# Another order of the turn in a fused linear-attention and gated-FFN layer

## The reference, cut to what matters

```
x: 16 x 512 tokens x 256 channels, float32                      (16 blocks)
qkv = relu(x @ Wqkv.T)          q, k, v: 32 heads of 8 channels
vk  = per head: [v, 1].T @ k over the tokens of a block
num, den = vk applied to q ;    att = num / (den + 1e-15)
x1  = layernorm(x + att @ Wproj.T + bias)
h   = silu(x1 @ (Wg/127).T) * (x1 @ (Wu/127).T)       hidden 768
out = layernorm(x1 + h @ (Wd/127).T)
```

## Time and profile before

| | |
|---|---|
| median of the runs | 548.8 us |
| the profiled execution | 549.34 us |
| its span, first to last instruction | 547.5 us |
| mean granted TensorE clock | 0.998 |
| busy PE / DVE / ACT / POOL | 533.1 / 392.7 / 221.4 / 80.4 us |
| chain that ended last | PE 93%, DVE 4%, ACT 1% |
| DMA | 29.04 MB, mean 53 GB/s |

### The profile page before, as it was taken

How to read it: one execution, slowest core, us unless ns; L and a number is a source line. 1 busy time by engine, 2 the same in 40 slices (tenths; PEclk the granted TensorE clock), 3 DMA queues, 4 the chain that set the end, 5 groups by cost and what they waited for, 6 DMA issues and landing times.

```text
span 547.5 us, 9297 instructions
## 1 busy us (share of the span) xinstructions
PE 533.1 (97%) x3531; PEld 465.8 (85%) x3531; DVE 392.7 (72%) x885; ACT 221.4 (40%) x376; POOL 80.4 (15%) x94
## 2 busy tenths in 40 slices
PE   8889999999999999999999999999999999999995
PEld 4777989898898988989898898988989898898975
DVE  5777858587684957858587684957858587684976
ACT  3365243442525435243542524435243542524431
POOL 2001110011100111110011100111110011100212
PEclk9999999999999999999999999999999999999999
DMA  8400120202112030121202112030121202102011
GB/s 296 166 0 3 40 78 29 87 0 77 38 38 77 0 112 3 38 77 31 84 0 77 38 38 77 0 110 5 38 77 37 78 0 77 38 0 79 1 40 40
DMA packets 8653, 29.04 MB, mean 53 GB/s; under 512 B 960, under 2 KB 1728, under 8 KB 8640
## 3 DMA queue, kind: packets, MB, share of 16 engines
q1 hardware_dynamic: 8640, 28.85, 14.8%
HBM read 20.46 MB, written 8.39 MB: 53 GB/s over the span
## 4 chain that ended last, share of the span: by engine, by line
PE 93%; DVE 4%; ACT 1%; issue 1%; DMA 1%; POOL 0%; POOLq 0%; SPq 0%
PE abcd_ps L585 45%; PE gate_ps L585 17%; PE up_ps L585 16%; PE abcd_ps L625 6%; PE abcd_ps L633 5%; PE abcd_ps L614 3%; DMA wq_raw<-w_q 1%; DVE x1T_lo L337 0%; PE abcd_ps L732 0%; DVE h L344 0%; ACT silu L241 0%; DVE st L567 0%; DVE st L400 0%; DVE r L563 0%; DVE att L377 0%
## 5 line engine op out<-in xcount | busy, mean ns | idle before, releaser
L344 DVE SCALAR_TENSOR_TENSOR h<-up_ps,silu 128x512 f32<-128x512 f32 x96 | 66.1, 688 | 79.1 <-ACT silu L241 79.1
L241 ACT ACTIVATE silu<-gate_ps 128x512 f32<-128x512 f32 x96 | 57.4, 597 | 98.3 <-PE gate_ps L585 98.3
L585 PE MATMUL abcd_ps<-wd_hi,h_hi 128*128 128x256 f32 x384 | 93.1, 283 | 0.8 <-DVE h_lo L337 0.8
L585 PE MATMUL abcd_ps<-wd_hi,h_lo 128*128 128x256 f32 x384 | 92.9, 283 | 0.0
L585 PE MATMUL gate_ps<-x1T_hi,wg_hi 128*128 128x512 f32 x192 | 79.4, 414 | 2.0 <-DVE x1T_lo L337 1.9
L337 DVE TENSOR_TENSOR h_lo<-h,h_hi 128x512 fp32r<-128x512 f32 x96 | 66.1, 689 | 14.4 <-ACT h_hi L236 11.2
L585 PE MATMUL up_ps<-x1T_hi,wu_hi 128*128 128x512 f32 x192 | 75.1, 391 | 0.0
L585 PE MATMUL up_ps<-x1T_lo,wu_hi 128*128 128x512 f32 x192 | 75.0, 391 | 0.0
L585 PE MATMUL gate_ps<-x1T_lo,wg_hi 128*128 128x512 f32 x192 | 74.9, 390 | 0.0
L585 PEld LDWEIGHTS abcd_ps<-wd_hi,h_hi 128*128 128x128 f32 x384 | 73.7, 192 | 1.1 <-DVE h_lo L337 1.0
L585 PEld LDWEIGHTS abcd_ps<-wd_hi,h_lo 128*128 128x128 f32 x384 | 73.7, 192 | 0.0
(11 more groups left out here) (119 smaller groups left out, 945.2 us busy)
## 6 DMA issues: line engine op xcount, KB each, us to landing
x_raw<-x_tok SPq DMA_DIRECT2D x16, 512.0 KB, 3.2
xT_raw<-x_chan SPq DMA_DIRECT2D x15, 512.0 KB, 3.3
out<-out_sb SPq DMA_DIRECT2D x15, 512.0 KB, 2.6
wg_raw<-w_gate SPq DMA_DIRECT2D x1, 768.0 KB, 6.3
wu_raw<-w_up SPq DMA_DIRECT2D x1, 768.0 KB, 7.8
wd_raw<-w_down SPq DMA_DIRECT2D x1, 768.0 KB, 9.1
xT_raw<-x_chan SPq DMA_DIRECT2D x2, 256.0 KB, 3.6
wkv_raw<-w_kv SPq DMA_DIRECT2D x1, 512.0 KB, 5.5
```

Source lines behind the costliest of these rows:

```text
L241: nc.scalar.activation(silu[:, j % 2, :], gate_ps[j % 2][:], ACT.Silu, scale=WSCALE).then_inc(silu_ok[j], 1)
L344: nc.vector.scalar_tensor_tensor(out=h[:, j, :], in0=up_ps[j % 2][:], scalar=WSCALE, in1=silu[:, j % 2, :], op0=ALU.mult, op1=ALU.mult).th ...
L585: last = mm(dst, lhsT, rhs, start=start and n == 0, stop=stop and n == len(pairs) - 1)
```

## The change

PE does in turn i: pieces 0 to 3, the transposes of att, pieces 4 and 5, proj, q and all four kv tiles of block i+1, the first half of down, vk of block i+1, the second half of down, the transposes of x1, num of block i+1. So vk and num of a block are now made at the end of the turn before. Down sums into `gate_ps[1]` and `up_ps[1]`, q into A and B, kv into CC, D, A, B, x1T into `gate_ps[0]` and `up_ps[0]`. A piece j from 2 on waits for `silu_ok[j-2]` ahead of its gate products and for `h_ok[j-2]` only ahead of its up products. x1 is normalised in place in r1, transposed from there, and SP copies r1 to x1 with a transfer, for which the next `r1_of` waits. DVE's order follows: the output of block i-2 is written inside the FFN half, the low part of x transposed between h of tiles 2 and 3, the low parts of h of tiles 2 and 3 after those of att, those of 4 and 5 after r1. The four signals per kind for the last block's token tiles become one counter each.

```diff
@@ sync
+            def turn(i):
+                any_i = not isinstance(i, int)
+                if any_i or i >= 2:
+                    sp.wait_ge(out_ok, i - 1)
+                    sp.dma_start(out[i - 2], out_sb[:].rearrange("p t c -> p (t c)")).then_inc(stored, 16)
+                if any_i or i + 1 < NB:
+                    sp.wait_ge(xb_ok, i + 1)
+                    sp.dma_start(x_raw[:], x[i + 1]).then_inc(x_in, 16)
+                if any_i or i + 2 < NB:
+                    load_xT(i + 2)
+                if any_i or 0 < i < NB - 1:
+                    sp.wait_ge(r2_ok[1], i)
+                    sp.dma_start(x1[:], r1[:]).then_inc(x1_copied, 16)
@@ vector
             def r1_of(b, pairs=False):
+                if not isinstance(b, int) or b > 1:
+                    dve.wait_ge(x1_copied, 16 * (b - 1))
...
+            def ffn_half(i):
+                att_of(i)
+                h_of(i - 1, 0)
+                if not isinstance(i, int) or i > 1:
+                    out_of(i - 2)
+                h_of(i - 1, 1)
+                h_lo_of(i - 1, 0, 1)
+                h_of(i - 1, 2)
+                if not isinstance(i, int) or i < NB - 1:
+                    xT_lo_of(i + 1)
+                h_of(i - 1, 3)
+                attT_lo_of(i)
                 h_lo_of(i - 1, 2, 3)
                 h_of(i - 1, 4, 5)
+            def attention_half(i):
                 r1_of(i)
                 dve.wait_ge(st1_ok, i + 1)
+                h_lo_of(i - 1, 4)
+                aggregated(st1, mv1, mv1_ok)
+                h_lo_of(i - 1, 5)
+                x1_of(i, r1)
                 r2_add(i - 1, 0, x1)
                 dve.wait_ge(r2_ok[0], i)
                 stats(st2, r2, 0)
+                vk_of(i + 1)
                 r2_add(i - 1, 1, x1)
                 dve.wait_ge(r2_ok[1], i)
                 stats(st2, r2, 1, st2_ok)
                 dve.wait_ge(st2_ok, i)
+                x1T_lo_of(i)
                 aggregated(st2, mv2, mv2_ok)
@@ tensor, gate_up
                     if j >= 2:
-                        pe.wait_ge(h_ok[j - 2], b + 1)
+                        pe.wait_ge(silu_ok[j - 2], b + 1)
+                    if j == 1 and (not isinstance(b, int) or b > 0):
+                        pe.wait_ge(r2_ok[0], b)
+                        pe.wait_ge(r2_ok[1], b)
...
                     add_up(gate, gate_hi[:-1], stop=False)
+                    if j >= 2:
+                        pe.wait_ge(h_ok[j - 2], b + 1)
                     add_up(up, up_hi[:-1], stop=False)
@@ tensor
+            def ffn_half(i):
+                gate_up(i - 1, 0, 1, 2, 3)
                 attT_of(i)
                 gate_up(i - 1, 4, 5)
                 proj_of(i)
+            def attention_half(i):
+                pe.wait_ge(xT_lo_ok, i + 2)
+                q_of(i + 1)
+                for t, bank in enumerate((CC, D, A, B)):
+                    if t < 2:
+                        pe.wait_ge(r1_ok[t], i + 1)
+                    else:
+                        pe.wait_ge(q_ok[t - 2], i + 2)
+                    kv_of(t, i + 1, bank)
+                down_of(i - 1, (0, 1))
+                vk_of(i + 1)
+                down_of(i - 1, (2, 3))
+                x1T_of(i, r1)
+                num_of(i + 1)
```

More of the change, by code:

```diff
@@ L101, in build @@
         A, B, CC, D = (abcd[:, n, :] for n in range(4))
+        down_ps = (gate_ps[1][:], up_ps[1][:])
         num_ps = abcd[:, :, 0:KC * NW].rearrange("p t (k n) -> p t k n", k=KC)
@@ L130, in build @@
         rstd1_pair, x1_pair = signals("rstd1_pair", 2), signals("x1_pair", 2)
-        down_tile, r2_tile, st2_tile = signals("down_tile", NT), signals("r2_tile", NT), signals("st2_tile", NT)
-        mv2_tile, ve2_tile = signals("mv2_tile", NT), signals("ve2_tile", NT)
-        rstd2_tile, out_tile = signals("rstd2_tile", NT), signals("out_tile", NT)
+        down_tile, r2_tile, st2_tile, mv2_tile, ve2_tile, rstd2_tile, out_tile = (
+            signal(f"{n}_tile") for n in ("down", "r2", "st2", "mv2", "ve2", "rstd2", "out"))
         last_down = [bank[:, :C] for bank in (A, B, CC, D)]
@@ L173, in _ @@
             sp.dma_start(wd_raw[:], down_w).then_inc(wd_in, 16)
[L174 to L178, removed]
+            turn(0)
+            turn(1)
+            with sp.Fori(2, NB - 2) as i:
+                turn(i)
+            turn(NB - 2)
+            turn(NB - 1)
+            turn(NB)
             for t in range(NT):
-                sp.wait_ge(out_tile[t], 1)
+                sp.wait_ge(out_tile, t + 1)
                 sp.dma_start(out[NB - 1][:, t * C:(t + 1) * C], out_last[:, t, :]).then_inc(stored, 16)
@@ L268, in attT_hi_of, with x1T_hi_of @@
                 T_hi_of(b, attT_mm, attT_hi, attT_hi_ok, (A, B))
-            def x1T_hi_of(b, banks=(CC, D)):
+            def x1T_hi_of(b, banks=(gate_ps[0][:], up_ps[0][:])):
                 T_hi_of(b, x1T_mm, x1T_hi, x1T_hi_ok, banks)
@@ L390, in attT_lo_of, with x1T_lo_of @@
                 T_lo_of(b, attT_hi_ok, attT_lo_ok, attT_hi, attT_lo, (A, B))
-            def x1T_lo_of(b, banks=(CC, D)):
+            def x1T_lo_of(b, banks=(gate_ps[0][:], up_ps[0][:])):
                 T_lo_of(b, x1T_hi_ok, x1T_lo_ok, x1T_hi, x1T_lo, banks)
@@ L427, in r2_add @@
                 nc.vector.scalar_tensor_tensor(
-                    out=pair(r2, n), in0=(A, B)[n], scalar=WSCALE, in1=pair(x1_of_b, n), op0=ALU.mult, op1=ALU.add).then_inc(r2_ok[n], 1)
+                    out=pair(r2, n), in0=down_ps[n], scalar=WSCALE, in1=pair(x1_of_b, n), op0=ALU.mult, op1=ALU.add).then_inc(r2_ok[n], 1)
             def normed(dst, r, mv, rs, ok, tiles=range(NT)):
@@ L440, in out_of @@
             def out_of(b):
+                if not isinstance(b, int) or b > 0:
+                    dve.wait_ge(stored, 16 * b)
                 dve.wait_ge(rstd2_ok, b + 1)
@@ L504, in second_part @@
                 dve.wait_ge(st2_ok, i)
-                x1_of(i, x1)
+                x1T_lo_of(i)
                 aggregated(st2, mv2, mv2_ok)
[L507 to L524, removed]
-            i = NB - 1
[L528 to L537, removed]
+            for i in (1, 2):
+                ffn_half(i)
+                attention_half(i)
+            with dve.Fori(3, NB - 1) as i:
+                ffn_half(i)
+                attention_half(i)
+            i = NB - 1
+            ffn_half(i)
             h_lo_of(i - 1, 4, 5)
@@ L638, in attT_of, with x1T_of @@
                 transposed(att, (A, B), attT_mm)
-            def x1T_of(b, src, banks=(CC, D)):
+            def x1T_of(b, src, banks=(gate_ps[0][:], up_ps[0][:])):
                 pe.wait_ge(x1_ok, b + 1)
@@ L689, in down_of @@
             def down_of(b, tiles=range(NT)):
+                pe.wait_ge(h_ok[NH - 1], b + 1)
                 for t in tiles:
[L691 removed]
+                    last = down_part(b, t, range(NH), down_ps[t // 2][:, (t % 2) * C:(t % 2 + 1) * C])
                     if t % 2:
                         last.then_inc(down_mm[t // 2], 1)
[L695 to L718 removed]
+            def ffn_half(i):
+                gate_up(i - 1, 0, 1, 2, 3)
                 attT_of(i)
@@ L793, in _ @@
                     for t in (2 * n, 2 * n + 1):
-                        last = nc.tensor.transpose((CC, D)[k][:, t * P:(t + 1) * P],
+                        last = nc.tensor.transpose((A, B)[k][:, t * P:(t + 1) * P],
                                                    x1_last[:, t, k * P:(k + 1) * P], ident)
```

100 lines of the change are left out of this document (28 added, 72 removed).

## The result

The changed kernel is slower, by less than a per cent: a median of 554.2 us in nine runs (552.24 to 557.0) against 549.2 for the kernel before (547.83 to 551.16 in nine), a ratio of 1.0086 with a 95% interval of 1.0066 to 1.0106, so 3.6 to 5.8 us. The forecast was 552.2, +3.4; the range held it, and the sign was right. One execution of experiment 1, 664.14 us at a mean granted clock of 0.755, is left out of that run's ratio.

A forecast was written before the change was run, and what follows sets the result against it. PE, busy in all of a 32.83 us turn, was taken as the bound. Seams -2.5, wait of piece 0 +5.7 and ends +0.2 gave +3.4 on the median 548.8: 552.2 us, range 546.3 to 556.6.

The forecast's parts named there:

- The wait of piece 0: PE waits for x1T_lo behind num until 3.07 after the x1 transposes start (T): 0.41 us per turn, +5.7 us.
- The seams: PE's losses at products behind plain float32 groups: x1T and num share one, vk's gets narrower; -2.5 us in all.
- one seam for two: x1T and num stand together on PE, saving one loss of 0.13 in each of 14 turns, -1.8 us.
- The sign that was named: On PE, three first products of 0.5 us per turn and not four would show the saved seams.
- Rival 3: Seams don't merge, since the stop at piece 0 replaces them: 554.7 us, 1.1% slower, chance 0.10.
- The upper one of the wait: Upper bound at piece 0: 0.6 per turn (+8.4), if num ran at 0.117 per product with no hand-over.
- Slack 0.25. No cost: At proj: attT_lo lets it start at 14.73, PE arrives at 14.98; slack was 0.65 before; no cost, but tightest.
- Rival 1: Proj waits as well, the DVE and ACT chain from den to attT_lo being late: +3.9, 556.1 us, chance 0.17.
- Rival 2: No wait at piece 0, num being slower or the low part earlier: 546.5 us, 0.4% faster, chance 0.17.
- Rival 4: The clock falls from transposes, num and the stop in a row each turn: 576 us, chance 0.02.
- The copy, the normalisation in place, the queues: SP's transfer of r1 to x1, x1 normalised in place, and SP and POOL order: no cost, 0.
- The ends: Last turn: r1 later, +0.5; last block's fifth piece no longer waits for h, -0.3; together +0.2.

The follow-up runs named there:

- experiment 1: Changed kernel with DVE's low part of x transposed moved behind attT_lo: turn 33.059 us, ratio 1.0062 to the kernel before.
- 9 with the move of 1: Changed kernel, x1 transposes between the last two down tiles, x1T_lo ahead of the second r2 add, low part of xT behind attT_lo: turn 32.700 us, ratio 0.9958.
- 3: Changed kernel with DVE's aggregates of r2 and a tiny memset ahead of x1T_lo instead of behind: turn 33.321 us, ratio 1.0114 to the kernel before.
- 8: Changed kernel, x1T_lo ahead of the second r2's statistics, low part of xT behind attT_lo, POOL's bias add later: turn 32.884 us, ratio 1.0013.
- 6: Changed kernel with one more 128x128 transpose per turn, between the second and third kv tile: turn 33.346 us, ratio 1.0122 to the kernel before.
- 2: Changed kernel with POOL's bias add started at the first rounded part of attT instead of behind den: turn 33.070 us, ratio 1.0060.
- 9 without the move of 1: Changed kernel, x1 transposes between the last two down tiles, x1T_lo ahead of the second r2 add, low part of xT unmoved: turn 32.845 us, ratio 1.0000.
- 7: Changed kernel without the transfer of r1 to x1 and its wait, so later blocks' residual is an old x1: turn 33.193 us, ratio 1.0077.
- 5: Kernel before with only the relaxed wait (silu ahead of gate products, h ahead of up products): turn 32.826 us, ratio 0.9988.
- 4: Changed kernel with the old wait, h of two tiles earlier ahead of the gate products too: turn 33.366 us, ratio 1.0141 to the kernel before.

## Why the prediction was right, point by point

PE's turn by stretches, each from its first start to that of the next (us, means of the fourteen turns; the columns are the kernel before, the changed one, and experiments 1 and 9 with the move of 1):

| stretch | before | after | 1 | 9 |
|---|---|---|---|---|
| x1 transposes | 0.790 | 0.872 | 0.872 | 0.792 |
| num | 1.865 | 2.183 | 2.182 | 1.863 |
| pieces 0 to 3 | 7.609 | 7.403 | 7.400 | 7.365 |
| transposes of att, pieces 4 and 5 | 4.529 | 4.553 | 4.529 | 4.530 |
| proj | 2.873 | 2.966 | 2.872 | 2.873 |
| q and kv | 8.318 | 8.187 | 8.188 | 8.187 |
| vk | 1.083 | 1.084 | 1.083 | 1.083 |
| down | 5.760 | 5.931 | 5.932 | 6.007 |

- **The wait of piece 0** is what makes the change slower. Its end was right to 0.02 (3.05), and its cause is shown by 3, 8 and 9. Its size was not: PE stands still for 0.31, since x1T and num behind it take 2.74 from T (8), not 2.66, and the pieces behind the stop take 0.04 more (7.40 against 7.365). That makes +0.35 per turn, 4.9 us, where the forecast had +0.41 and 5.7.
- **The seams** were priced at -0.18 per turn, 2.5 us. Take the stop and its 0.04 out of 1 and the new order has 33.06 - 0.35 = 32.71, which is -0.12, 1.7 us. The seam behind vk came out as priced (0.14 to 0.09), and 0.02 more was saved ahead of vk and behind num. But "one seam for two" gave 0.127 - 0.082 = 0.045 and not 0.13, since the last transpose then takes its full time (6). The sign that was named, three first products and not four, is there (0.50, 0.48 and, behind vk, a narrow 0.38). Rival 3, nothing saved, is out.
- **The two errors cancel, and not by chance alone.** Forecast -0.18 + 0.41, measured -0.12 + 0.35, both +0.23, so without the wait of proj the turn is 33.06 and 33.07 (1 and 2) against the 33.05 of the forecast (its own terms add up to 33.06). Both errors are mostly the same 0.08, the transposes read as 0.79 ahead of num: as DVE's chain fixes the start of piece 0, it doesn't matter for the sum how PE's time ahead of it is split into work and stop. That the rest cancels too is luck: 0.02 gained ahead of vk and behind num, 0.02 by which piece 0 came earlier than forecast, 0.04 lost behind the stop.
- **The bounds.** The upper one of the wait, 0.6 from num at 0.117 per product, doesn't follow: 16 x 0.117 is the 1.87 that the sum has.
- **Why a seam isn't free.** The prediction says that PE gets nothing ahead of it. The rule of the Trainium skill (TensorE: Matmul & The Clock Gate, Part 2, what happens when you issue a matmul), that weight loads are pulled ahead of running matmuls, isn't contradicted by the rows of 6: the load starts one instruction ahead there too, but that instruction starts only 0.03 before the product. That seams are free, as the prediction drew from the rule, doesn't hold: a seam behind transposes costs 0.13 by the starts, and of that 0.045 is left when the last transpose's time is taken out.
- **"Slack 0.25. No cost"** is the step that failed, and with it the 0.12 per turn, 1.7 us, by which +3.4 fell short of +5.0. The sum gave the output 1.30 until h1; it took 1.67 (212.68 to 214.35), which is 0.37 more than the sum and 0.12 more than the slack; 0.06 was made up ahead of it, so attT_lo comes 0.06 late in this turn. The prediction had seen that the second root now runs ahead of POOL's add and looked only at who waits for POOL, not at which DVE instruction would run beside the add: it starts 0.9 later behind den than before and meets the output. Before, the four products of att and h ran beside it, which read PSUM. Rival 1, with a chance of 0.17 and 3.9 us for 0.3 late in 13 turns, is what happened, in a small form: late by 0 to 0.06 and 0.09 of a restart, together 1.7 us. So the measured time is the forecast's mechanism and rival 1's together.
- **Rival 2** (no wait at piece 0) would have needed 0.4 us, and didn't come; it would have been worth 0.12 per turn, not 0.18.
- **Rival 4**: the granted clock is 1.00 in the window of the turn; the low clock of the profiled execution lies in the prologue, and a kernel with the old order had it too. But the earlier trace rows, one execution, say less than the prediction took from them: in the profiles of 1 and of 9 without the move of 1 the clock was 0.67 and 0.66 from 40 to 45 us, right behind this same stretch of transposes and a stop of 1.57. At the lower level products of width 512 start 0.43 apart, not 0.23, so the price per product was right.
- **The copy, the normalisation in place, the queues**: costed at 0. For the copy 7 shows no cost; the other two weren't tested by themselves, but the differences in the table are accounted for without them.
- **The ends**: x_last +0.36 against +0.5; from the last block's piece 0 to the end 23.26 (530.74 to 554.0) against 23.55 before (523.95 to 547.5), so -0.3 as forecast, and 5 has it with the relaxed wait alone (525.63 to 548.9, 23.27).
- **The relaxed wait** was costed at nothing in the turns. Against the kernel before that is right (5), but without it the new order would be another 0.19 per turn slower (4). It was part of the change's price: the prediction looked at the new waits, which pass, and not at what the old one would cost in the new order.

## What to carry to other kernels

Where one engine is busy all the time, a new order is worth its seams, and these are small against any wait: all that the new order saved there was 1.7 us, and the stop ahead of piece 0 took 4.9 and that of proj 1.7. So put behind each producer at least as much work as the whole chain through the other engines takes, and move the step whose consumer is tightest away from the end of the turn, not only its neighbour. When a step changes its time, look also at what it runs beside. A price read from start to start hangs on what stands behind: the same eight transposes read 0.79 and 0.87. Count waits by the distance between starts, and in the weight loads' list, since PE's own list missed all of these.

## What the hardware showed that I had not expected

- DVE stands still beside a POOL instruction that reads SBUF, when its own two inputs are both in SBUF: two low parts of h take 2.54 us instead of 1.28, the low part of xT 2.47 instead of 1.21. So does the output, which reads one tensor and two values per partition from SBUF: 1.76 instead of 1.38. Instructions with an input in PSUM kept their time, and so did the reciprocal of den (0.95), whose one input is in SBUF, though it had begun before POOL did. POOL's add took 2.38 to 2.43 in the turns with or without DVE beside it.
- Between a plain float32 transpose and a split product behind it there are 0.03 us from start to start, and 0.11 to another plain product; the split product of width 512 then takes 0.31 to the next start instead of 0.23. Together, 0.34 is close to 0.11 + 0.23: most of what looks like a price of the change-over is the last transpose itself.
- The granted clock went down early in six of thirteen profiles, in either order of the work. In four it was 0.77 to 0.85 in the window from 20 to 30 us, and in these PE had just stood 1.79 to 2.21 us for the low part of the second x block; in the other nine that stop was 0.96 to 1.69. In two of these nine (1, and 9 without the move of 1) it was 0.66 to 0.67 from 40 to 45 us, behind stops of 1.64 and 1.57 that all thirteen have. The prologue's work is the same in all of them. The length of the first stop differs with how the first transfers happened to land, and what decides whether the clock falls isn't shown.
